# Moving the decoder bias of a fused attention and mixture-of-experts layer from a matmul to a VectorE add

## The chip, the cores and the metric

The kernel runs on one core of a Trainium2 chip. The metric is the device time of one execution in microseconds; of three runs the median counts. A profile of one further execution shows every instruction of every engine.

## The reference, cut to what matters

The layer takes `x` of 2 x 4096 tokens with 512 channels, normalizes it, and adds to `x` the output of a linear attention and that of a feed-forward branch with eight experts. The change concerns the end of the feed-forward branch:

```
moe_out = jnp.einsum('ned,ne->nd', eo, comb)
rates = jax.nn.sigmoid(moe_out @ c2s_w + c2s_b)
dec = jax.nn.sigmoid(x @ dec_w + dec_b)        # x is rates: 1024 -> 512
mu = jnp.mean(dec, axis=-1, keepdims=True)
var = jnp.var(dec, axis=-1, keepdims=True)
return (dec - mu) * jax.lax.rsqrt(var + 1e-05) * ln_g + ln_b
```

The bias `dec_b` runs along the 512 output channels, which lie in the free dimension of the output tile. The kernel computes both sigmoids as tanh of half the argument, so what it adds ahead of the second tanh is twice `dec_b` plus the sum of the decoder's weight rows. It has this row on all 128 partitions, once, at the start of the stage.

## The kernel before

Tokens are worked on in 16 blocks of 512 (four token tiles of 128). Four stages follow each other: `front` (A: normalization, encoder, router), `keyvalue` (B), `experts` (C) and `decode` (D). All matmuls of float32 data are done in passes over a high and a low part, so that one product is three matmuls. Each engine has its own instruction list, written out by hand, and waits on semaphores; nothing is reordered by a scheduler.

In `decode`, which the change touches, TensorE does for block i: four query projections (`query`, into banks `bX`), the transpose of the expert mixture (`middle`, L1443, waits for `mo`), content-to-rate products (`rates`, L1452 and L1453, into bank `bY`, wait for `midl`), the attention denominators, then the attention output of block i-1 (`attend`), then the decoder of block i: four bias matmuls (`decoder_bias`, L1494), and eight rounds `decoder(i, k)` of twelve matmuls into four banks `bD[t]`, between which stand `rates` for later rounds and the fan-out of the denominators (`fan`). The bias matmul multiplies a 128x128 selector by `rows`, a tile in which the high part of the bias row lies in partition 64 and its low part in partition 96.

ScalarE moves the queries (`q`, L1362, and `qh`, L1365), the mixture's high part (`midh`, L1370), the rates, and at the end of a block the four decoder banks with tanh into `out[:, t, :]` (L1421). VectorE does the low parts (`ql` L1564, `midl` L1569, `ratel` L1574), the shares `q` and `qnl` (L1609, L1614), the mixture of block i+1 (`half` L1548, `mo` L1555), and for block i-1 the statistics (`stats`, L1579 and L1584), the normalization (`norm` L1589), the residual (`add` L1597) and the sum with the attention output (`attend` L1604). Its order is that of the loop over blocks at the end of `decode`: the mixture of block i+1 is the last piece of block i's round, and the statistics of block i the first of the next. GpSimd gathers expert outputs and computes the inverse deviation; SyncE issues the loads and stores.

At the end of stage C, VectorE copies constants for stage D (L1260 to L1263).

Of the kernel before, what the change touches and what calls it, by code (L numbers as in the profile page):

```python
# [12 lines left out]
P = 128  # L13
# [94 lines left out]
def place(nc):  # L108
# [22 lines left out]
    put("CcD", "c2s", [P, HID], F32R)  # L131
    put("CcD", "fan", [P, KC, P], F32R)
    put("CcD", "rc2", [P, BLK], F32R)
    put("CcD", "rows", [P, BLK], F32R)
    put("CcD", "pick_bias", [P, P], F32R)
    put("CcD", "ln_g", [P, DIM])
    put("CcD", "bias", [P, DIM])
    for s in range(BATCH):
# [80 lines left out]
    put("Cc", "c2s_raw", [P, HID])  # L219
    put("Cc", "fanf", [P, KC, P])  # L220
    put("Cc", "blank", [P, BLK])
    put("Cc", "pbf", [P, P])
    put("Cc", "onesf", [MOE, BLK])
    put("Cc", "bias2", [P, 2, DIM])

# [3 lines left out]
    put("D", "rateh", [P, 3, BLK], F32R)  # L229
    put("D", "ratel", [P, 3, BLK], F32R)  # L230
    put("D", "out", [P, NT, DIM])
    put("D", "q", [P, KC, BLK])
    put("D", "qh", [P, 2, BLK], F32R)
    put("D", "ql", [P, 2, BLK], F32R)
# [796 lines left out]
def experts(nc, d, T, S):  # L1031
    with ExitStack() as ctx:
# [59 lines left out]

        @block.gpsimd
        def _(pool):
            fanf, pbf = T["fanf"], T["pbf"]
            pool.memset(T["onesf"][:, :], 1.0).then_inc(S["c_consts"], 1)
            pool.wait_ge(S["c_consts"], 1)
            pool.memset(T["blank"][:, :], 0.0).then_inc(S["c_consts"], 1)
            pool.memset(fanf[:, :, :], 0.0).then_inc(S["c_consts"], 1)
            pool.memset(pbf[:, :], 0.0).then_inc(S["c_consts"], 1)  # L1100
            pool.wait_ge(S["c_consts"], 4)
            pool.memset(fanf[0:MOE, :, :], 1.0).then_inc(S["c_consts"], 1)
            for k, row in enumerate((64, 96)):
                pool.wait_ge(S["c_consts"], 5 + k)
                pool.memset(pbf[row:row + 1, :], 1.0).then_inc(S["c_consts"], 1)
            n = 7
            for half in range(2):
                v = fanf[32 * half:32 * half + 32, :, :]
                for cm, st, base in ((-HD, 1, 0), (HD, -1, HD - 1)):
                    pool.wait_ge(S["c_consts"], n)  # L1110
                    pool.affine_select(out=v, in_=v, compare_op=ALU.is_ge, fill=0.0, base=base,
                                       pattern=[[st * P, KC], [st, P]], channel_multiplier=cm)\
                        .then_inc(S["c_consts"], 1)
                    n += 1
            pool.wait_ge(S["c_consts"], 11)
            pool.wait_ge(S["vec_in"], 32)
            pool.tensor_tensor(T["bias"][:, :], T["bias2"][:, 0, :], T["bias2"][:, 1, :], ALU.add)

# [101 lines left out]
        @block.vector  # L1220
        def _(dve):
            close_products(dve, T, S, 1)
            turn_dve(dve, T, S, 1, bY)
            dve.wait_ge(S["c_consts"], 1)
            for i in range(2):
                dve.tensor_copy(cl[MOE:P, i, :], T["onesf"][:, :]).then_inc(S["cl_ones"], 1)

            def content(g):
                dve.wait_ge(S["ch_out"], g + 1)
                if g >= 2:  # L1230
                    dve.wait_ge(S["e1_done"], (g - 2) * EC + EC)
                dve.tensor_tensor(cl[0:MOE, g % 2, :], bT[0:MOE, :], f32(ch[0:MOE, g % 2, :]), ALU.subtract)\
                    .then_inc(S["cl_out"], 1)

            def close_tile(g):
                dve.wait_ge(S["tout_done"], g + 1)
                wait(dve, S[f"eo_stored{g % 3}"], 16 * (g // 3))
                dve.tensor_reduce(yo[g % 3][:, :, :], bY[:, :].rearrange("p (t h c) -> p t c h", t=NT, h=2), AX.X, ALU.add)\
                    .then_inc(S["yo_out"], 1)

            for g in range(KC):
                project_dve(dve, T, S, 0, 1, g, bH[g])
            content(0)
            for n in range(LAST + LAG):
                g, j = divmod(n, EC)
                if j == 0 and g + 1 < NS:
                    content(g + 1)
                if n < LAST:
                    dve.wait_ge(S["hidh_out"], n + 1)
                    wait(dve, S["e2_done"], n - 3)  # L1250
                    dve.scalar_tensor_tensor(out=hidl[:, n % 4, :], in0=bH[n % 4][:, :], scalar=0.0,
                                             in1=f32(hidh[:, n % 4, :]), op0=ALU.max, op1=ALU.subtract)\
                        .then_inc(S["hidl_out"], 1)
                if j == 1 and g >= 2:
                    close_tile(g - 2)
                if j == 2 and g == 1:
                    close_denominators(dve, T, S, 0, 1)
                if j == 3 and g == 1:
                    dve.wait_ge(S["c_consts"], 11)
                    dve.tensor_copy(T["fan"][:, :, :], T["fanf"][:, :, :])  # L1260
                    dve.tensor_copy(T["pick_bias"][:, :], T["pbf"][:, :])
                    dve.tensor_copy(T["rc2"][:, :], T["blank"][:, :])
                    dve.tensor_copy(T["rows"][:, :], T["blank"][:, :]).then_inc(S["d_consts"], 1)  # L1263
                if j == 3 and 2 <= g < 2 + len(DEC):
                    name, c = DEC[g - 2]
                    dve.wait_ge(S["wh_out"], W_DEC + g - 1)
                    dve.tensor_tensor(T[name + "_l"][:, c, :], T[name + "_raw"][:, c, :], f32(T[name + "_h"][:, c, :]),
                                      ALU.subtract).then_inc(S["wl_out"], 1)
                if j == 3 and g == 16:
                    dve.wait_ge(S["wh_out"], W_C2S + 1)  # L1270
                    dve.tensor_tensor(T["c2s"][MOE:P, :], T["c2s_raw"][MOE:P, :], f32(T["c2s"][MOE:P, :]), ALU.subtract)\
                        .then_inc(S["wl_out"], 1)
            for g in range((LAST + LAG - 2) // EC - 1, NS):
                close_tile(g)
# [4 lines left out]
def decode(nc, d, T, S, out_dram):  # L1279
    with ExitStack() as ctx:  # L1280
# [4 lines left out]
        q, qh, ql, qnh, qnl = (T[n] for n in ("q", "qh", "ql", "qnh", "qnl"))  # L1285
        x = [T["xd0"], T["xd1"]]
        ga, gb, half, mo, midh, midl = (T[n] for n in ("ga", "gb", "half", "mo", "midh", "midl"))
        dlow, dsum, rc, rc2, rows = (T[n] for n in ("dlow", "dsum", "rc", "rc2", "rows"))

        block = ctx.enter_context(nc.Block())  # L1290

# [65 lines left out]
        def _(act):  # L1357
# [34 lines left out]
            for i in range(NB):  # L1392
# [22 lines left out]
                    if 3 <= k < 3 + KC:  # L1415
                        share(i, k - 3)
                for t in range(NT):
                    act.wait_ge(S["dec_done"], i * NT + t + 1)
                    if i:
                        act.wait_ge(S[f"stored{t}"], 16 * i)  # L1420
                    act.activation(out[:, t, :], bD[t][:, :], ACT.Tanh, scale=0.25).then_inc(S["dec_out"], 1)  # L1421

        @block.tensor
        def _(pe):
# [62 lines left out]
                    k = pe.matmul(bD[0][:, :], one, T["dec_l"][:, c, :], start=False, stop=(c == HC - 1))  # L1487
                k.then_inc(S["dec_summed"], 1)

            def decoder_bias(i, t):  # L1490
                if i == 0:
                    pe.wait_ge(S["rows_out"], 2)
                wait(pe, S["dec_out"], i * NT)
                pe.matmul(bD[t][:, :], T["pick_bias"][:, :], rows[:, :], start=True, stop=False)  # L1494

            def decoder(i, k):
                n = i * HC + k
                pe.wait_ge(S["ratel_out"], n + 1)
                for t in range(NT):
                    o = slice(t * P, (t + 1) * P)  # L1500
                    pe.matmul(bD[t][:, :], rateh[:, n % 3, o], T["dec_h"][:, k, :], start=False, stop=False)  # L1501
                    pe.matmul(bD[t][:, :], rateh[:, n % 3, o], T["dec_l"][:, k, :], start=False, stop=False)  # L1502
                    m = pe.matmul(bD[t][:, :], ratel[:, n % 3, o], T["dec_h"][:, k, :], start=False, stop=(k == HC - 1))  # L1503
                    if k == HC - 1:
# [4 lines left out]
            for i in range(NB + 1):  # L1509
# [20 lines left out]
                    for t in range(1, NT):  # L1530
                        attend(i - 1, t)
                if ahead:
                    for t in range(NT):
                        decoder_bias(i, t)
                    for k in range(HC):
                        decoder(i, k)
                        if k + 2 < HC:
                            rates(i, k + 2)
                        if 3 <= k < 3 + KC:
                            fan(i, k - 3)  # L1540

        @block.vector
        def _(dve):
# [27 lines left out]
            def rates(i, k):  # L1571
                n = i * HC + k
                dve.wait_ge(S["rateh_out"], n + 1)
                dve.tensor_tensor(ratel[:, n % 3, :], rate[:, k % 2, :], f32(rateh[:, n % 3, :]), ALU.subtract)\  # L1574
                    .then_inc(S["ratel_out"], 1)

            def stats(i, t):
                dve.wait_ge(S["dec_out"], i * NT + t + 1)
# [37 lines left out]
            def decoder_sum():  # L1616
                dve.wait_ge(S["dec_summed"], 1)
                dve.wait_ge(S["vec_in"], 48)
                dve.scalar_tensor_tensor(out=out[:, 0, :], in0=out[:, 1, :], scalar=2.0, in1=bD[0][:, :],
                                         op0=ALU.mult, op1=ALU.add).then_inc(S["dec_biased"], 1)  # L1620
                dve.wait_ge(S["dec_biased"], 1)
                dve.tensor_copy(rows[64:P, :], out[64:P, 0, :]).then_inc(S["rows_out"], 1)
                dve.wait_ge(S["rows_out"], 1)
                dve.tensor_tensor(rows[96:P, :], out[96:P, 0, :], f32(rows[96:P, :]), ALU.subtract)\
                    .then_inc(S["rows_out"], 1)

            for m in range(KC):
                query(0, m)
# [5 lines left out]
            for i in range(NB + 1):  # L1634
# [42 lines left out]
                if ahead:  # L1677
                    for k in range(HC):
# [6 lines left out]
                        if 3 <= k < 3 + KC:  # L1685
                            share(i, k - 3)
                            share_low(i, k - 3)
                        if k == HC - 1 and i + 1 < NB:
                            mixture(i + 1)


def build(nc, d, out_dram):
# [70 lines left out]
```

## Time and profile before

| what | us |
|---|---|
| three runs | 2024.8, 2026.44 (median), 2026.93 |
| the profiled execution | 2028.13 |
| its span, first to last instruction | 2026.4 |
| TensorE matmuls busy | 1965.3 (97%) |
| VectorE busy | 1045.1 (52%) |
| ScalarE busy | 814.9 (40%) |
| GpSimd busy | 392.9 (19%) |

The mean granted TensorE clock is 0.991 of full. Stage D begins near 1155 us. Busy shares are averages over stages; what bounds a stage is read from who waits for whom in it. A matmul's duration overlaps that of the next one, so what a matmul takes of TensorE's time is the distance of starts. "Idle before" in square brackets is the time that the engine stood still ahead of an instruction, with what released it.

### The profile page before, as it was taken

What the parts mean: (1) busy time and instruction counts of PE and PEld (TensorE: products, weight loads), DVE (VectorE), ACT (ScalarE), POOL (GpSimd) and SP (SyncE); (2) the same over time, 40 slices, a digit from 0 to 9 for tenths busy, and PEclk for the clock granted to TensorE, in tenths of its full rate; (3) what the DMA queues carried; (4) which work ended last, traced back from release to release, by engine and by line L of the source; (5) the groups of instructions that cost most, each with busy time, mean ns of one, the idle gap of its engine ahead of it and who ended that gap; (6) DMA issues with size and microseconds to landing.
All of it is one profiled execution on the core that took longest, in us unless ns stands there. A gap on an engine that the chain in (4) does not pass through costs nothing. (4 is left out here: it accounts for less than half of the span.)

```text
span 2026.4 us, 25149 instructions
## 1 busy us (share of the span) xinstructions
PE 1965.3 (97%) x9100; PEld 1609.1 (79%) x9100; DVE 1045.1 (52%) x1846; ACT 814.9 (40%) x1359; POOL 392.9 (19%) x428
## 2 busy tenths in 40 slices
PE   7999999999899999998899989999999999999998
PEld 5888888888788888887678768888888888888886
DVE  5445455553442222222888645555556556566554
ACT  4444445444221222112677533444344443444442
POOL 1000000000003444431000122222222222222220
PEclk9999999999999999999999989999999999999999
DMA  5561324423112233321877512222222222222210
GB/s 200 209 236 69 141 90 145 169 89 122 69 65 99 110 112 113 112 107 54 317 232 236 187 49 89 89 88 89 88 88 88 88 88 78 73 78 78 84 66 34
DMA packets 74826, 233.95 MB, mean 115 GB/s; under 512 B 9856, under 2 KB 15952, under 8 KB 68176
## 3 DMA queue, kind: packets, MB, share of 16 engines
q1 hardware_dynamic: 66432, 219.58, 30.7%
q0 software_dynamic: 8272, 12.76, 2.2%
q8 instruction: 73, 1.20, 0.2%
q14 instruction: 49, 0.40, 0.1%
HBM read 151.95 MB, written 80.36 MB: 115 GB/s over the span
## 5 line engine op out<-in xcount | busy, mean ns | idle before, releaser
L569 DVE TENSOR_TENSOR spl<-sp_t,sph 128x512 fp32r<-128x512 f32 x128 | 88.6, 692 | 240.1 <-ACT sph L391 240.1
L103 PE MATMUL A_E<-xs,enc_h 128*128 128x512 f32 x512 | 206.8, 404 | 0.0
L105 PE MATMUL A_E<-xs,enc_h 128*128 128x512 f32 x512 | 200.8, 392 | 0.0
L1574 DVE TENSOR_TENSOR ratel<-rate,rateh 128x512 fp32r<-128x512 f32 x128 | 88.5, 691 | 217.4 <-ACT rateh L1384 177.4
L104 PE MATMUL A_E<-xs,enc_l 128*128 128x512 f32 x512 | 200.6, 392 | 0.0
L1501 PE MATMUL D_D<-dec_h,rateh 128*128 128x512 f32 x512 | 199.8, 390 | 0.0
L1502 PE MATMUL D_D<-dec_l,rateh 128*128 128x512 f32 x512 | 199.8, 390 | 0.0
L1503 PE MATMUL D_D<-dec_h,ratel 128*128 128x512 f32 x512 | 199.5, 390 | 0.0
L1376 ACT ACTIVATE rate<-D_Y,cols 128x512 f32<-128x512 f32 x128 | 87.9, 687 | 264.3 <-PE D_Y L1453 261.5
L387 ACT ACTIVATE sp_t<-A_E,cols 128x512 f32<-128x512 f32 x128 | 88.1, 688 | 245.4 <-PE A_E L105 245.4
L863 POOL DMA_INDIRECT slots_scratch<-ctok,idx x128 | 123.8, 967 | 249.3 <-DVE v L991 123.4
L1333 POOL DMA_INDIRECT ga<-eo_scratch,idx x64 | 66.4, 1037 | 371.5 <-DVE ratel L1574 192.4
L991 DVE SCALAR_TENSOR_TENSOR v<-B_KV,v 128x512 fp32r<-128x512 f32 x64 | 44.3, 692 | 174.9 <-ACT v L892 174.8
L892 ACT ACTIVATE v<-B_KV 128x512 fp32r<-128x512 f32 x64 | 38.4, 600 | 204.8 <-PE B_KV L940 204.8
L1346 POOL TENSOR_TENSOR xd<-xd,bias 128x512 f32<-128x512 f32 x64 | 80.5, 1283 | 176.2 <-DVE out L1604 176.2
L105 PEld LDWEIGHTS A_E<-xs,enc_h 128*128 128x128 f32 x512 | 96.5, 189 | 21.6
L1502 PEld LDWEIGHTS D_D<-dec_l,rateh 128*128 128x128 f32 x512 | 96.2, 188 | 20.6
L1503 PEld LDWEIGHTS D_D<-dec_h,ratel 128*128 128x128 f32 x512 | 96.1, 188 | 20.5
L1501 PEld LDWEIGHTS D_D<-dec_h,rateh 128*128 128x128 f32 x512 | 96.3, 188 | 20.3
L103 PEld LDWEIGHTS A_E<-xs,enc_h 128*128 128x128 f32 x512 | 96.8, 189 | 19.0 <-issue 0.4
L104 PEld LDWEIGHTS A_E<-xs,enc_l 128*128 128x128 f32 x512 | 97.0, 189 | 18.6
L985 DVE SCALAR_TENSOR_TENSOR kl<-B_KV,kh 128x512 fp32r<-128x512 f32 x64 | 44.3, 692 | 128.5 <-ACT kh L888 128.5
(283 smaller groups left out, 4810.3 us busy)
## 6 DMA issues: line engine op xcount, KB each, us to landing
xs_scratch<-xs SPq DMA_DIRECT2D x16, 2048.0 KB, 9.3
xsd<-xs_scratch SPq DMA_DIRECT2D x16, 2048.0 KB
xs<-xs_scratch SPq DMA_DIRECT2D x14, 2048.0 KB, 8.5
wt<-ew_scratch SPq DMA_DIRECT2D x39, 513.0 KB, 3.8
x<-in_x SPq DMA_DIRECT2D x16, 1024.0 KB, 5.9
xd<-in_x SPq DMA_DIRECT2D x16, 1024.0 KB
out_y<-out SPq DMA_DIRECT2D x64, 256.0 KB, 2.1
slots_scratch<-zt SPq DMA_DIRECT2D x1, 9984.0 KB
```

Of the source, the lines that this page charges most:

```text
L103: pe.matmul(out, w_hi, x_hi, start=start, stop=False)
L104: pe.matmul(out, w_lo, x_hi, start=False, stop=False)
L105: return pe.matmul(out, w_hi, x_lo, start=False, stop=stop)
L387: act.activation(T["sp_t"][:, m % 2, :], bE[m % 2][:, :], ACT.Tanh, bias=T["enc_b"][:, m:m + 1], scale=0.5).then_inc(S["sp_out"], 1)
L569: dve.tensor_tensor(T["spl"][:, n % 3, :], T["sp_t"][:, m % 2, :], f32(T["sph"][:, n % 3, :]), ALU.subtract)\
L863: pool.indirect_dma_start(d["slots"][:, :], bass.IndirectOffsetOnAxis(ap=T["idx2" if second else "idx1"][:, t:t + 1], axis=0), T["ctok"][: ...
L1346: pool.tensor_tensor(x[i % 2][:, t, :], x[i % 2][:, t, :], T["bias"][:, :], ALU.add)\
L1376: act.activation(rate[:, k % 2, :], bY[:, :], ACT.Tanh, bias=T["c2s_b"][:, k:k + 1], scale=0.5)\
L1501: pe.matmul(bD[t][:, :], rateh[:, n % 3, o], T["dec_h"][:, k, :], start=False, stop=False)
L1502: pe.matmul(bD[t][:, :], rateh[:, n % 3, o], T["dec_l"][:, k, :], start=False, stop=False)
L1503: m = pe.matmul(bD[t][:, :], ratel[:, n % 3, o], T["dec_h"][:, k, :], start=False, stop=(k == HC - 1))
L1574: dve.tensor_tensor(ratel[:, n % 3, :], rate[:, k % 2, :], f32(rateh[:, n % 3, :]), ALU.subtract)\
```

## The change

The four bias matmuls of each block go. The first decoder matmul of each bank now starts the accumulation (`start=(k == 0)`), and waits until VectorE has emptied the bank for the block before. VectorE adds the bias row `dec_row` (128x512, the same row on all partitions) while it moves the bank into `out[:, t, :]` (`decoded`), and ScalarE's tanh reads and writes `out[:, t, :]` in SBUF. The wait for the store of the block before moves from ScalarE to VectorE with the write. `decoder_sum` writes `dec_row` in one operation; the two that split the row go, and so do the tiles `rows` and `pick_bias` and what fills them in stage C.

```
-            def decoder_bias(i, t):
-                if i == 0:
-                    pe.wait_ge(S["rows_out"], 2)
-                wait(pe, S["dec_out"], i * NT)
-                pe.matmul(bD[t][:, :], T["pick_bias"][:, :], rows[:, :], start=True, stop=False)
...
+                    if k == 0:
+                        if i:
+                            pe.wait_ge(S["biased"], (i - 1) * NT + t + 1)
+                        elif t == 0:
+                            pe.wait_ge(S["row_out"], 1)
-                    pe.matmul(bD[t][:, :], rateh[:, n % 3, o], T["dec_h"][:, k, :], start=False, stop=False)
+                    pe.matmul(bD[t][:, :], rateh[:, n % 3, o], T["dec_h"][:, k, :], start=(k == 0), stop=False)
...
+            def decoded(i, t):
+                dve.wait_ge(S["dec_done"], i * NT + t + 1)
+                if i == 0:
+                    dve.wait_ge(S["row_out"], 1)
+                else:
+                    dve.wait_ge(S[f"stored{t}"], 16 * i)
+                dve.tensor_tensor(out[:, t, :], bD[t][:, :], T["dec_row"][:, :], ALU.add).then_inc(S["biased"], 1)
...
-                    act.wait_ge(S["dec_done"], i * NT + t + 1)
-                    if i:
-                        act.wait_ge(S[f"stored{t}"], 16 * i)
-                    act.activation(out[:, t, :], bD[t][:, :], ACT.Tanh, scale=0.25).then_inc(S["dec_out"], 1)
+                    act.wait_ge(S["biased"], i * NT + t + 1)
+                    act.activation(out[:, t, :], out[:, t, :], ACT.Tanh, scale=0.25).then_inc(S["dec_out"], 1)
...
-                dve.scalar_tensor_tensor(out=out[:, 0, :], in0=out[:, 1, :], scalar=2.0, in1=bD[0][:, :],
-                                         op0=ALU.mult, op1=ALU.add).then_inc(S["dec_biased"], 1)
-                dve.wait_ge(S["dec_biased"], 1)
-                dve.tensor_copy(rows[64:P, :], out[64:P, 0, :]).then_inc(S["rows_out"], 1)
-                dve.wait_ge(S["rows_out"], 1)
-                dve.tensor_tensor(rows[96:P, :], out[96:P, 0, :], f32(rows[96:P, :]), ALU.subtract)\
-                    .then_inc(S["rows_out"], 1)
+                dve.scalar_tensor_tensor(out=T["dec_row"][:, :], in0=out[:, 1, :], scalar=2.0, in1=bD[0][:, :],
+                                         op0=ALU.mult, op1=ALU.add).then_inc(S["row_out"], 1)
...
-                        if k == HC - 1 and i + 1 < NB:
-                            mixture(i + 1)
+                        if k == HC - 1:
+                            if i + 1 < NB:
+                                mixture(i + 1)
+                            for t in range(NT):
+                                decoded(i, t)
...
-                    dve.tensor_copy(T["pick_bias"][:, :], T["pbf"][:, :])
-                    dve.tensor_copy(T["rc2"][:, :], T["blank"][:, :])
-                    dve.tensor_copy(T["rows"][:, :], T["blank"][:, :]).then_inc(S["d_consts"], 1)
+                    dve.tensor_copy(T["rc2"][:, :], T["blank"][:, :]).then_inc(S["d_consts"], 1)
```

On VectorE, at the end of a block's round and the start of the next one, this is the order before (`half` and `mo` are the mixture, `st` and `mv` the statistics, `midl` the low part that TensorE's `rates` needs):

```order
L1614 TENSOR_TENSOR qnl<-q,qnh 128x512
L1548 TENSOR_SCALAR half<-ga,w_60 128x64 x4
L1555 SCALAR_TENSOR_TENSOR mo<-gb,w_61,half 128x128 x4
L1579 BN_STATS st<-out 128x6 x4
L1582 MEMSET held 128x1
L1584 BN_AGGR mv<-st 128x2 x4
L1589 SCALAR_TENSOR_TENSOR out<-out,mv,ln_g 128x512
L1564 TENSOR_TENSOR ql<-q,qh 128x512
L1569 TENSOR_TENSOR midl<-D_Y,midh 128x512
```

And the same place after the change (line numbers have moved by a few):

```order
L1609 TENSOR_TENSOR qnl<-q,qnh 128x512
L1535 TENSOR_SCALAR half<-ga,w_60 128x64 x4
L1542 SCALAR_TENSOR_TENSOR mo<-gb,w_61,half 128x128 x4
L1570 TENSOR_TENSOR out<-D_D,dec_row 128x512 x4
L1574 BN_STATS st<-out 128x6 x4
L1577 MEMSET held 128x1
L1579 BN_AGGR mv<-st 128x2 x4
L1584 SCALAR_TENSOR_TENSOR out<-out,mv,ln_g 128x512
L1551 TENSOR_TENSOR ql<-q,qh 128x512
L1556 TENSOR_TENSOR midl<-D_Y,midh 128x512
```

Four adds from the banks stand between the mixture and the statistics; the rest keeps its order.

On TensorE, where the attention output of block i-1 ends and the decoder of block i begins, before:

```order
L1478 MATMUL D_X<-mh_78,qnh 128x512
L1479 MATMUL D_X<-ml_79,qnh 128x512
L1480 MATMUL D_X<-mh_78,qnl 128x512
L1494 MATMUL D_D<-rows,pick_bias 128x512 x4
L1501 MATMUL D_D<-dec_h,rateh 128x512
```

And after:

```order
L1468 MATMUL D_X<-mh_76,qnh 128x512
L1469 MATMUL D_X<-ml_77,qnh 128x512
L1470 MATMUL D_X<-mh_76,qnl 128x512
L1490 MATMUL D_D<-dec_h,rateh 128x512
L1491 MATMUL D_D<-dec_l,rateh 128x512
```

The four matmuls of `rows` and `pick_bias` are gone, and the first decoder round follows the attention output directly.

## Rows read from the trace of the kernel before

**Rows 1.** Waits of TensorE in stage D: us in total, times, longest us.

```profile
PE D_Y L1452 <- DVE midl L1569: 9.7, 16, 1.4
PE D_X L1478 <- DVE out L1604: 4.7, 1, 4.7
PE D_Y L1443 <- DVE mo L1555: 3.8, 1, 3.8
```

**Rows 2.** TensorE in order of time, at a block boundary: start us, us, what.

```profile
1432.80 0.50 PE L1452 MATMUL D_Y<-midh,c2s 128*128 128x512 f32 x1 [0.56 <-DVE midl L1569]
```

**Rows 3.** VectorE in order of time, at the same boundary.

```profile
1425.53 0.69 DVE L1614 TENSOR_TENSOR qnl<-q,qnh 128x512 fp32r<-128x512 f32 x1 [0.70 <-ACT qnh L1390]
...
1426.79 1.13 DVE L1555 SCALAR_TENSOR_TENSOR mo<-gb,w,half 128x128 f32<-128x128 f32 x4
1427.84 2.47 DVE L1579 BATCH_NORM_STATS2 st<-out 128x6 f32<-128x512 f32 x4
...
1432.07 0.68 DVE L1569 TENSOR_TENSOR midl<-D_Y,midh 128x512 fp32r<-128x512 f32 x1
1432.67 0.73 DVE L1597 SCALAR_TENSOR_TENSOR out<-out,rs,xd 128x512 f32<-128x512 f32 x1
```

**Rows 4.** ScalarE in order of time, at the same boundary.

```profile
1425.40 2.04 ACT L1421 ACTIVATE out<-D_D 128x512 f32<-128x512 f32 x4
...
1430.21 0.58 ACT L1370 ACTIVATE midh<-D_Y 128x512 fp32r<-128x512 f32 x1
```

**Rows 5.** TensorE in order of time, at the bias matmuls of two blocks.

```profile
1187.81 1.91 PE L1494 MATMUL D_D<-rows,pick_bias 128*128 128x512 f32 x4
1189.52 0.51 PE L1501 MATMUL D_D<-dec_h,rateh 128*128 128x512 f32 x1
...
1399.46 1.07 PE L1494 MATMUL D_D<-rows,pick_bias 128*128 128x512 f32 x4
1400.37 0.39 PE L1501 MATMUL D_D<-dec_h,rateh 128*128 128x512 f32 x1
```

**Rows 6.** VectorE in order of time, last block, two adds from a bank.

```profile
2015.19 1.28 DVE L1604 TENSOR_TENSOR out<-D_X,out 128x512 f32<-128x512 f32 x2
```

**Rows 7.** TensorE in order of time, at three longer waits.

```profile
964.12 0.47 PE L1193 MATMUL C_H<-ch,wt 128*128 128x512 f32 x1 [1.61 <-issue]
...
1171.58 0.50 PE L1460 MATMUL D_Y<-qh,den 128*128 128x512 f32 x1 [2.21 <-DVE ql L1564]
...
1172.61 0.55 PE L1486 MATMUL D_D<-dec_h,ones 128*128 128x512 f32 x1
...
2015.93 0.79 PE L1478 MATMUL D_X<-mh,qnh 128*128 128x512 f32 x1 [4.70 <-DVE out L1604]
2016.52 0.63 PE L1479 MATMUL D_X<-ml,qnh 128*128 128x512 f32 x1
```

**Rows 8.** Stretches: A:B length, busy us by engine, granted clock, DMA share, GB/s.

```profile
2016.00:2019.00 3.00, 3.00 (x7) 2.41 (x8) 0.48 (x1) 0.00 (x0) 0.00 (x0) 0.50 0.47 175
...
1172.70:1176.00 3.30, 3.30 (x10) 2.53 (x9) 0.00 (x0) 0.00 (x0) 0.00 (x0) 0.50 0.98 415
...
964.00:967.00 3.00, 2.08 (x10) 1.44 (x10) 1.09 (x3) 1.70 (x4) 0.00 (x0) 1.00 1.04 406
```

**Rows 9.** VectorE and TensorE in order of time: constants' copies, bias row split.

```profile
975.48 0.21 DVE L1261 CAST pick_bias<-pbf 128x128 fp32r<-128x128 f32 x1
975.62 0.42 DVE L1262 CAST rc<-blank 128x512 fp32r<-128x512 f32 x1
975.95 0.41 DVE L1263 CAST rows<-blank 128x512 fp32r<-128x512 f32 x1
...
977.61 0.50 PE L1202 MATMUL C_O<-hidh,wt 128*128 128x512 f32 x1 [0.92 <-DVE hidl L1251]
...
1178.33 0.42 DVE L1622 CAST rows<-out 64x512 fp32r<-64x512 f32 x1
1178.79 0.69 DVE L1624 TENSOR_TENSOR rows<-out,rows 32x512 fp32r<-32x512 f32 x1
```

More of the change, by code:

```diff
@@ L133, in place @@
     put("CcD", "rc2", [P, BLK], F32R)
-    put("CcD", "rows", [P, BLK], F32R)
-    put("CcD", "pick_bias", [P, P], F32R)
     put("CcD", "ln_g", [P, DIM])
@@ L221, in place @@
     put("Cc", "blank", [P, BLK])
-    put("Cc", "pbf", [P, P])
     put("Cc", "onesf", [MOE, BLK])
@@ L231, in place @@
     put("D", "out", [P, NT, DIM])
+    put("D", "dec_row", [P, DIM])
     put("D", "q", [P, KC, BLK])
@@ L1094, in _ @@
         def _(pool):
-            fanf, pbf = T["fanf"], T["pbf"]
+            fanf = T["fanf"]
             pool.memset(T["onesf"][:, :], 1.0).then_inc(S["c_consts"], 1)
@@ L1099, in _ @@
             pool.memset(fanf[:, :, :], 0.0).then_inc(S["c_consts"], 1)
-            pool.memset(pbf[:, :], 0.0).then_inc(S["c_consts"], 1)
-            pool.wait_ge(S["c_consts"], 4)
+            pool.wait_ge(S["c_consts"], 3)
             pool.memset(fanf[0:MOE, :, :], 1.0).then_inc(S["c_consts"], 1)
[L1103 to L1106, printed above, removed]
+            n = 4
             for half in range(2):
@@ L1114, in _ @@
                     n += 1
-            pool.wait_ge(S["c_consts"], 11)
+            pool.wait_ge(S["c_consts"], 8)
             pool.wait_ge(S["vec_in"], 32)
@@ L1258, in _ @@
                 if j == 3 and g == 1:
-                    dve.wait_ge(S["c_consts"], 11)
+                    dve.wait_ge(S["c_consts"], 8)
                     dve.tensor_copy(T["fan"][:, :, :], T["fanf"][:, :, :])
-                    dve.tensor_copy(T["pick_bias"][:, :], T["pbf"][:, :])
-                    dve.tensor_copy(T["rc2"][:, :], T["blank"][:, :])
-                    dve.tensor_copy(T["rows"][:, :], T["blank"][:, :]).then_inc(S["d_consts"], 1)
+                    dve.tensor_copy(T["rc2"][:, :], T["blank"][:, :]).then_inc(S["d_consts"], 1)
                 if j == 3 and 2 <= g < 2 + len(DEC):
@@ L1287, in decode @@
         ga, gb, half, mo, midh, midl = (T[n] for n in ("ga", "gb", "half", "mo", "midh", "midl"))
-        dlow, dsum, rc, rc2, rows = (T[n] for n in ("dlow", "dsum", "rc", "rc2", "rows"))
+        dlow, dsum, rc, rc2 = (T[n] for n in ("dlow", "dsum", "rc", "rc2"))
         block = ctx.enter_context(nc.Block())
@@ L1532, in _ @@
                 if ahead:
-                    for t in range(NT):
-                        decoder_bias(i, t)
                     for k in range(HC):
```

## Prediction

> **What bounds the kernel now.** I read the table of engines, then the waits of TensorE in the last stage, then one block boundary in order of time on TensorE, VectorE and ScalarE, and last the stretches of half clock. TensorE is busy nearly everywhere; in the last stage, where the change is, it waits in few places [rows 1]. Sixteen times it waits for VectorE's `midl` (9.7 us in all), once 3.8 us for `mo` (first block) and once 4.7 us for `out` (after the last block). Inside a block its stream has no holes. So a matmul taken out of the stream gives its whole period back, and anything that makes `midl` later is paid in full, because TensorE already stands there with nothing in hand.
>
> At the boundary of blocks 4 and 5 TensorE has drained its projections and waits 0.56 us before the first content-to-spike matmul L1452 at 1432.80 [rows 2]. It waits for `midl`, which VectorE starts at 1432.07 and ends at 1432.75 [rows 3]. Before that VectorE runs without a pause from 1425.53: the last `qnl`, the mixture, four `bn_stats`, aggregation, `norm`, `ql`, `midl`. ScalarE is no rival releaser: `midh`, the input of `midl`, ends at 1430.79 [rows 4], 1.28 us before `midl` starts. What holds `midl` back is VectorE's own queue. The other boundaries repeat this, with waits of about 0.6 us (9.7 us less the first block's 1.4, over 15).
>
> **What is removed.** The four bias matmuls at the start of a block's decoder. They take from 1399.46 to 1400.37, 0.91 us, or 0.227 us each, since matmuls overlap and the 0.39 us of one is not its price [rows 5]. Fifteen blocks give 15 x 0.91 = 13.6 us; the first block's four run at half clock, from 1187.81 to 1189.52, and give 1.7. Nothing else on TensorE changes: the first decoder matmul of a tile now opens the sum. Removed: 15.3 us.
>
> The Trainium skill, page "TensorE: Matmul & The Clock Gate", section "Back-to-back issue gap", gives about 131 ns as the sustained spacing of matmuls with 512 columns. By it 64 of them would be an estimated 8.4 us and the sum would come out 6.9 us later; the trace disagrees with its 227 ns, and the trace has these very matmuls, so the measurement decides.
>
> **What is added.** Four VectorE adds a block, bank and SBUF row in, `out` tile out, put behind the mixture and ahead of the next block's work. Their nearest row is the add L1604, which reads a bank and a tile of the same shape: two of them back to back take 1.28 us, one alone 0.69, so they start 0.59 to 0.60 us apart [rows 6]. Four move everything behind them by 4 x 0.60 = 2.40 us. Bounds from the rows: a 128x512 copy starts 0.34 us after the one ahead of it [rows 9] (four: 1.36 us), and 0.73 us is the `scalar_tensor_tensor` behind `midl`, close to an unoverlapped 0.69 (four: 2.9 us). I take 2.40.
>
> The Trainium skill, page "VectorE: DVE Perf Modes", section "The DRAIN you can't avoid", has it that the next operation does not start until the pipeline of the one before is empty. By that rule the four adds would be 4 x 0.69 = 2.76 us, an estimate, and fifteen boundaries would be 5.4 us more; the two adds in 1.28 us speak against it.
>
> Can anything cover the 2.40 us? The adds could have begun earlier, since three of the four tiles are summed before the last `qnl` ends, but in VectorE's order they stand behind the mixture, where the engine has not one idle slice before `midl`. Their inputs are long ready, so no new wait for TensorE enters. Behind them are queued the four statistics, which now wait for a tanh that waits for an add. The first tanh starts about 0.7 us after the first add, takes 0.6 and is done about 1.1 us before the first statistic's turn, so the round trip costs nothing more. ScalarE has the four tanhs, until now done at 1427.4, held to about 1431.0 on the same scale; then come `q`, `qh` and `midh`, which ends near 1432.7, still 1.8 us ahead of where `midl` now starts (1434.47). ScalarE stays off the path. The waits on `stored` move from ScalarE to VectorE; they name stores issued behind the attention output of the block before, ahead of the whole decoder, and are long fulfilled.
>
> So at each of 15 boundaries TensorE's wait of 0.56 us becomes 2.96 us: +2.40 x 15 = +36.0 us. Everything in a block shifts with its start, so the 0.91 us won does not shorten the wait.
>
> **What the longer wait does to the clock.** After a wait of 4.70 us in the last block the granted clock is 0.50 (1.2 GHz), and 7 matmuls take 3.00 us, 0.43 each [rows 7, 8]; after one of 2.21 us it fell too, though only 1.0 us after work had begun again; after one of 1.61 us it stayed at 1.00 (2.4 GHz). The 0.56 us waits never cost it. A half-clock stretch costs: from 2016 to 2019, 7 matmuls x (0.43 - 0.227) = 1.4 us, with its edges about 1.5. A wait of 2.96 us lies above the 2.21 that did it and below 4.70. I take 12 of 15 boundaries, as where the wait falls seems to matter: 12 x 1.5 = +18 us. Bounds: none, and 15 x 1.7 = 25.
>
> **The ends.** First block: the two operations that split the bias row (1178.33 and 1178.79 [rows 9]) go, together 1.2 us of the chain that TensorE's 3.8 us wait hangs on: -1.2. In the last block the 4.7 us wait for `out` grows by the same four adds: +2.4; its half-clock stretch may last a little longer (0 to 1.5). In the expert stage two constant copies go, 0.14 and 0.34 us apart from their neighbours, just ahead of a 0.92 us wait [rows 9]: at most -0.5, I take -0.3. The three small fills on GpSimd are off the path.
>
> **Sum**, against the profiled execution (2028.13 us, span 2026.4 and 1.7 around it): -15.3 + 36.0 + 18.0 - 1.2 + 2.4 - 0.3 = +39.6, so 2067.7. The median of the runs is 2026.44, 1.7 below the profiled one; the median forecast is 2066 us.
>
> **Rivals.**
> *The clock holds.* The wait grows as said, but at 2.96 us the half clock comes rarely. For it: the last stage shows no wait between 2.21 and 3.8 us, so the price at 2.96 is not seen. Then -15.3 + 36.0 - 1.2 + 2.4 - 0.3 = +21.6: 2048 us. Chance 0.2.
> *The clock stays low longer.* In the first block, waits of 3.8 and 1.4 us [rows 1] stand close together, and the bias matmuls at 1187.81 behind both still ran at half clock [rows 5]. If each boundary cost two stretches, another 15 x 1.5 = 22 us, or if the adds do not overlap (+5): 2070 to 2090, with a middle of 2084. Against it: TensorE has 10 us of unbroken matmuls right behind the wait. Chance 0.12.
> *The adds are covered (the other side).* One mechanism: VectorE's queue up to `midl` has room, so the adds fit in where it idles for `qnh` (0.70 us before 1425.53). It decides where the four adds delay `midl` by less than the 0.91 us that the matmuls give back, 0.23 us an add, which is under even the 0.34 us of a copy. Wholly covered it would give 2026.4 - 15.3 - 1.5 = 2010 us. Against it: the written order, which puts them behind `qnl`. Chance 0.06.
> *A draw.* A cover of some 1.5 us a boundary and no clock loss lands within 0.2% (4 us, about what can be told from no change): 0.03.
>
> **How the numbers follow.** Forecast 0.59, clock holds 0.2, clock low longer 0.12, covered 0.06, draw 0.03. The likeliest case alone runs from 2056 (half of the boundaries lose the clock) to 2076 (all at 1.7, adds at 0.65). The range takes in the clock rival at 2048 with slack for cheaper adds, and the lower part of the slow rival: 2044 to 2080. Faster 0.06, same 0.03, slower 0.91.
>
> **What would show it.** In the changed kernel's profile: TensorE's wait for `midl` at 15 boundaries near 3.0 us, 45 us in all where it was 9.7; VectorE's adds 0.60 us apart right behind `mo`; `midh` done before `midl` starts; a block from decoder start to boundary 0.91 us shorter; stretches of granted clock 0.50 behind most boundaries, each 1.5 us dear; a last wait for `out` near 7.1 us. It would be wrong if the wait for `midl` stayed under 1.5 us, if ScalarE's `midh` or `qh` released VectorE there, or if the clock row stayed at 9 throughout.

## The result: 2.8% slower

The changed kernel takes 2082.96 us (median of five runs, 2081.44 to 2089.77) against 2026.93 us; the ratio is 1.028 with a 95% interval of 1.0263 to 1.0297. The forecast was 2066 us in a range of 2044 to 2080. The direction and the chain of causes were right; the time lies 3 us beyond the range, and one term of the sum was too small.

The waits of TensorE in stage D of the changed kernel (us in total, times, longest us) answer to [rows 1]:

```profile
PE D_Y L1442 <- DVE midl L1556: 45.5, 16, 3.0
PE D_X L1468 <- DVE out L1599: 7.0, 1, 7.0
...
PE D_Y L1433 <- DVE mo L1542: 2.5, 1, 2.5
```

The wait for `midl` went from 9.7 to 45.5 us, that for the last `out` from 4.7 to 7.0, that for the first `mo` from 3.8 to 2.5. These three differences are +35.8, +2.3 and -1.3 us; the forecast had +36.0, +2.4 and -1.2.

VectorE at one boundary of the changed kernel, in order of time, which answers to [rows 3]:

```profile
1437.26 0.69 DVE L1609 TENSOR_TENSOR qnl<-q,qnh 128x512 fp32r<-128x512 f32 x1 [0.70 <-ACT qnh L1382]
...
1438.52 1.13 DVE L1542 SCALAR_TENSOR_TENSOR mo<-gb,w,half 128x128 f32<-128x128 f32 x4
1439.57 2.47 DVE L1570 TENSOR_TENSOR out<-D_D,dec_row 128x512 f32<-128x512 f32 x4
1441.96 2.46 DVE L1574 BATCH_NORM_STATS2 st<-out 128x6 f32<-128x512 f32 x4
...
1446.18 0.68 DVE L1556 TENSOR_TENSOR midl<-D_Y,midh 128x512 fp32r<-128x512 f32 x1
```

From the end of the mixture to the first statistic there are now 1441.96 - 1439.57 = 2.39 us: the adds start 0.60 us apart. ScalarE's high part is no releaser, as forecast, with 1.8 us to spare:

```profile
1440.28 2.42 ACT L1411 ACTIVATE out<-out 128x512 f32<-128x512 f32 x4 [3.06 <-DVE out L1570]
...
1443.76 0.58 ACT L1362 ACTIVATE midh<-D_Y 128x512 fp32r<-128x512 f32 x1
```

What the forecast undersized stands behind the wait. TensorE at this boundary, and at the one before it, in order of time, answers to [rows 2, 7]:

```profile
1389.95 0.79 PE L1442 MATMUL D_Y<-midh,c2s 128*128 128x512 f32 x1 [2.94 <-DVE midl L1556]
1390.55 0.63 PE L1443 MATMUL D_Y<-midl,c2s 128*128 128x512 f32 x1
...
1395.67 0.61 PE L103 MATMUL D_X<-xsd,wq_h 128*128 128x512 f32 x1
1396.09 0.42 PE L104 MATMUL D_X<-xsd,wq_l 128*128 128x512 f32 x1
...
1446.92 0.50 PE L1442 MATMUL D_Y<-midh,c2s 128*128 128x512 f32 x1 [2.96 <-DVE midl L1556]
1447.25 0.56 PE L1443 MATMUL D_Y<-midl,c2s 128*128 128x512 f32 x1
...
1450.59 0.47 PE L105 MATMUL D_X<-xsd,wq_h 128*128 128x512 f32 x1
1450.90 0.40 PE L103 MATMUL D_X<-xsd,wq_h 128*128 128x512 f32 x1
```

At the second of them the clock falls just after work has begun again (the first matmul takes 0.50 us, the second 0.56), and 9 matmuls take 3.65 us, from 1447.25 to 1450.90, where 9 x 0.23 = 2.1 would do: 1.6 us lost. At the first the clock has fallen 0.65 us before TensorE resumes (already its first matmul takes 0.79 us), and 14 matmuls take 6.14 us, from 1389.95 to 1396.09, for 3.2: 2.9 us lost. The stretches (length, busy us of TensorE, its weight loads, VectorE, ScalarE, GpSimd, then the granted clock, DMA share, GB/s) say the same:

```profile
1336.00:1340.00 4.00, 4.00 (x18) 3.27 (x18) 3.96 (x7) 1.51 (x3) 0.00 (x0) 1.00 0.00 0
1390.00:1396.00 6.00, 6.00 (x14) 4.74 (x15) 4.58 (x7) 1.32 (x2) 0.00 (x0) 0.50 0.00 0
...
1447.40:1450.60 3.20, 3.20 (x10) 2.43 (x9) 3.16 (x6) 1.32 (x2) 0.00 (x0) 0.50 0.01 3
1451.00:1455.00 4.00, 4.00 (x19) 3.24 (x18) 1.19 (x2) 2.44 (x4) 0.00 (x0) 1.00 0.00 0
```

Behind 14 of the 15 boundaries the clock fell to 0.50, that is 1.2 GHz (the one near 1336 kept it); eight times in the short form, six in the long one: 8 x 1.6 + 6 x 2.9 = 30 us, where the forecast had 18. The starts of the `rates` matmuls at four successive boundaries (1335.81, 1389.95, 1446.92 and 1502.63 us) give the same prices: the block behind the boundary that kept the clock takes 54.1 us, the one behind a long stretch 57.0, the one behind a short stretch 55.7.

### The profile page after: what moved, and what is told of

The parts are those of the page before. It is cut to its first block and busy times, and to the rows that moved or that the text cites. A ratio compares the mean times of both kernels' runs of the same rounds, so it can differ in the third digit from the quotient of the medians.

```text
span 2081.2 us, 25098 instructions
## 1 busy us (share of the span) xinstructions
PE 1983.4 (95%) x9036; PEld 1620.5 (78%) x9036; DVE 1081.3 (52%) x1906; ACT 818.7 (39%) x1359; POOL 388.7 (19%) x425
## 5 line engine op out<-in xcount | busy, mean ns | idle before, releaser
L103 PE MATMUL D_X<-xsd,wq_h 128*128 128x512 f32 x256 | 112.1, 438 | 3.0 <-PEq L1030 3.0
```

What stands on the lines that cost most here:

```text
L103: pe.matmul(out, w_hi, x_hi, start=start, stop=False)
```

## The experiments

Where a ratio is given, it is to the kernel before on the same chip in the same series, with a 95% interval. Beside the time I give the length of stage D in the profile, from the first transpose of the mixture (L1443 before, L1433 after) to the end of the span. It leaves out the three earlier stages, whose end varied between 1179.6 and 1185.2 us in the profiles taken here: before 845.0 us, changed 899.7. Each of these lengths is good to 0.1 us. Where I give the length of a block, it is the distance between the starts of the first `rates` matmul at successive boundaries, averaged over the 14 such distances from the second block on.

**The wait filled with work (e1_fill).** Ten matmuls nobody needs keep TensorE busy ahead of the wait:

```
             def rates(i, k):
+                if k == 0 and i:
+                    pe.wait_ge(S["qn_out"], i * KC)
+                    for _ in range(10):
+                        pe.matmul(bR[:, :], T["wq_h"][:, 0, 0:P], xs[:, 0, 0, :], start=True, stop=True)
                 pe.wait_ge(S["midl_out"], i + 1)
```

> The changed kernel with 10 more matmuls of 512 columns on TensorE just ahead of the wait for midl, at each of the 15 boundaries, into the bank bR that the next denominators overwrite. They take 10 x 0.227 = 2.3 us of a wait of 2.96 us. Theory (the wait costs its own length, and about 32 us more are half clock behind it): VectorE's chain ends at the same time, TensorE's wait falls to about 0.7 us, and the clock stays at 1.00 behind the boundaries; only the clock's share goes: 2083 - 30 = about 2052 us. Rival A (the overrun over the forecast is contention of the four adds with the matmuls, or anything else on VectorE's side): no change, 2080 to 2085. Rival B (the ten matmuls are paid as work): 2083 + 34 = 2117.

Measured: 2053.2 us, 1.0126 (1.0104 to 1.0148); stage D 869.9 us. Ten more matmuls a boundary made the kernel 30 us faster. TensorE's waits of this run, where 15 of the 16 waits for `midl` are now 0.6 us long:

```profile
PE D_Y L1446 <- DVE midl L1560: 10.5, 16, 1.4
PE D_X L1472 <- DVE out L1603: 7.0, 1, 7.0
```

and two stretches of it, the first across one boundary, the second from the end of the first block's half clock to the last block, across all 15:

```profile
1389.00:1396.00 7.00, 6.40 (x28) 4.89 (x27) 6.33 (x11) 2.89 (x6) 1.80 (x2) 1.00 0.00 1
...
1195.30:2041.50 846.20, 832.77 (x3639) 674.90 (x3637) 521.91 (x890) 339.02 (x546) 224.01 (x212) 1.00 0.22 76
```

The clock column reads 1.00 in both. VectorE's chain is as late as in the changed kernel: a block takes 54.2 us here, and 54.1 there behind the one boundary that kept the clock. So it is the clock that gave the 30 us back: 899.7 - 869.9 = 29.8. Contention and "matmuls are paid as work" both fall as explanations.

**Fewer of them (e8_fill_six).** The same with `range(6)`.

> The changed kernel with 6 more matmuls ahead of the wait for midl, where the first such run had 10. Nothing on VectorE's side changes, so the boundary is as long; TensorE's own wait is about 2.96 - 6 x 0.23 = 1.6 us. Theory (the clock's loss hangs on how long TensorE stands still, and 1.6 us is not enough): full clock behind the boundaries, the same time as with ten, about 2053 us. Rival (it takes less than that, and ten matmuls only just sufficed): half clock behind most of them at 1.6 us each, 2070 to 2078 us.

Measured: 2052.15 us, 1.0125 (1.0108 to 1.0141); stage D 869.2 us.

```profile
PE D_Y L1446 <- DVE midl L1560: 24.5, 16, 1.6
...
1188.70:2035.00 846.30, 819.16 (x3579) 663.74 (x3578) 521.42 (x889) 338.84 (x546) 220.91 (x212) 1.00 0.22 76
```

Waits of 1.5 us at the boundaries (24.5 us less the first block's 1.4, over 15) left the clock at full: the second line is the stretch across all of them. The time is that of ten fillers.

**The removal alone (e2_no_add).** No `decoded`; the tanh reads the bank as before, and the bias is left out. TensorE's wait ahead of the first decoder matmul names the tanh instead of the add, here and in the kernels with fewer adds.

```
-                            for t in range(NT):
-                                decoded(i, t)
...
-                    act.wait_ge(S["biased"], i * NT + t + 1)
-                    act.activation(out[:, t, :], out[:, t, :], ACT.Tanh, scale=0.25).then_inc(S["dec_out"], 1)
+                    act.wait_ge(S["dec_done"], i * NT + t + 1)
+                    if i:
+                        act.wait_ge(S[f"stored{t}"], 16 * i)
+                    act.activation(out[:, t, :], bD[t][:, :], ACT.Tanh, scale=0.25).then_inc(S["dec_out"], 1)
```

> The changed kernel without the four adds: the bias row is left out of the decoder, and ScalarE's tanh reads the bank as before. This is the removal of the matmuls alone. Theory (a matmul in the full stream gives back its period of 0.227 us): 2027 - 15.3 - 1.3 = 2010 us, TensorE's waits for midl back at 0.6 us. Rival (a removed matmul is worth less, for instance 0.131 us, or its gain is lost in the wait for midl): 2017 to 2025 us.

Measured: 2014.5 us, 0.9944 (0.9922 to 0.9966); stage D 831.1 us. The time lies between the theory and the rival. By the ratio the gain is 11.3 us (6.9 to 15.8), less than the 16.6 expected. By the trace stage D is 845.0 - 831.1 = 13.9 us shorter, and the wait for `mo`, ahead of it, 1.3 us: together 15.2. A block shrinks from 52.7 to 51.8 us, by 0.90, which is four matmuls of 0.225. The waits for `midl` are exactly those of before, 9.7 us. The price of 0.227 us a matmul is borne out by the trace; the runs alone would not tell it from a somewhat smaller one.

**The addition alone (e4_before_adds).** The kernel before, and four adds at the same place that nobody reads:

```
-                        if k == HC - 1 and i + 1 < NB:
-                            mixture(i + 1)
+                        if k == HC - 1:
+                            if i + 1 < NB:
+                                mixture(i + 1)
+                            for t in range(NT):
+                                dve.wait_ge(S["dec_out"], i * NT + t + 1)
...
+                                dve.tensor_tensor(ql[:, t % 2, :], bD[t][:, :], T["ln_g"][:, :], ALU.add)\
+                                    .then_inc(S["spared"], 1)
```

> The kernel before, bias matmuls kept, with four further VectorE adds behind the mixture; each reads a decoder bank and writes a tile that nobody reads. This is the addition alone. Theory (the two parts add up): changed kernel + 15.3 + 1.3 = about 2099 us, waits for midl near 2.96 us, 15 of them; the clock share may differ by some 8 us, as it depends on where the waits fall. Rival (in the changed kernel it is the longer round trip add, tanh, statistics that costs, not the adds' place in VectorE's queue): here tanh does not wait for an add, so the wait stays well below 2.96 us and the time near 2060.

Measured: 2096.6 us, 1.0347 (1.0325 to 1.037); stage D 915.3 us.

```profile
PE D_Y L1452 <- DVE midl L1571: 45.4, 16, 3.0
PE D_X L1478 <- DVE out L1606: 7.1, 1, 7.1
```

The same 45 us of waits without any tanh waiting for an add; the clock fell at all 15 boundaries, at seven of them in the long form. The kernel also makes VectorE and TensorE wait for these adds before they reuse the tile and the bank. With four adds it is the place in VectorE's queue that costs, and removal and addition add up: 2096.6 - 2083.0 = 13.6.

**Two adds, one add, three adds (e3_two_adds, e3c_one_add, e3b_three_adds).** Only the first two, one or three tiles are moved by VectorE; the tanh of the others reads its bank:

```
+                    if t < 2:
+                        act.wait_ge(S["biased"], i * 2 + t + 1)
+                        act.activation(out[:, t, :], out[:, t, :], ACT.Tanh, scale=0.25).then_inc(S["dec_out"], 1)
+                        continue
...
-                            for t in range(NT):
+                            for t in range(2):
                                 decoded(i, t)
```

> The changed kernel with the add on two of the four token tiles only; the other two tiles get no bias, their tanh reads the bank. Theory (0.60 us of wait for each add, half clock only behind waits above some 2 us): wait for midl 0.56 + 1.20 = 1.76 us, clock at 1.00 behind nearly all boundaries: 2010 + 15 x 1.20 + 1.2 = about 2030 us. Rival (each add costs the same, the clock included, a straight line from no add to four): (2010 + 2083) / 2 = 2046 us.

> The changed kernel with the add on one token tile only; the other three get no bias. With two adds the wait was 1.95 us and 12 of 15 boundaries were followed by half clock. Theory (a wait well below 1.6 us leaves the clock alone): wait about 1.3 us, no half clock behind the boundaries, 2014.5 + 15 x 0.75 + 0.8 = about 2027 us. Rival (the clock falls behind any wait longer than the 0.56 us of before): 15 x 1.6 more, about 2050.

> The changed kernel with the add on three token tiles; the fourth gets no bias. Wait about 2.5 us. Theory (how long the clock stays down grows with the wait: with two adds 12 stretches of one length, with four adds 14, six of them twice as long): nearly all boundaries, one to four of them doubled: 2014.5 + 15 x 1.95 + 1.8 + 15 x 1.6 + 4 = about 2073 us. Rival (a stretch of half clock costs the same 1.5 us whatever the wait, and the changed kernel's doubled ones are chance): none doubled, about 2067.

Measured: 2055.4 us with two, 2056.6 with one, 2057.0 with three (stage D 872.0, 873.2 and 873.0). All three expectations missed, theory and rival alike: one add costs as much as three. The wait was 1.95 us with one add as with two, where 1.3 and 1.76 us had been expected; half clock followed that length too; and with three adds it came more rarely than with one. The waits for `midl`, of two, one and three adds in turn:

```profile
PE D_Y L1448 <- DVE midl L1562: 30.6, 16, 2.0
```

```profile
PE D_Y L1448 <- DVE midl L1562: 30.7, 16, 2.0
```

```profile
PE D_Y L1448 <- DVE midl L1562: 36.9, 16, 2.4
```

VectorE with one add, in order of time, shows why:

```profile
1380.25 0.69 DVE L1576 TENSOR_TENSOR out<-D_D,dec_row 128x512 f32<-128x512 f32 x1
1381.63 2.47 DVE L1580 BATCH_NORM_STATS2 st<-out 128x6 f32<-128x512 f32 x4 [0.70 <-ACT out L1412]
```

Behind the add VectorE stands idle for 0.70 us, until the tanh that waited for the add is done: 0.69 + 0.70 = 1.39 us for the round trip, less than which no number of adds on the first tiles can cost. With four adds the round trip lies under the other three. The wait of 0.56 + 1.39 = 1.95 us was followed by half clock at 12 of 15 boundaries with two adds, at 13 with one, in the short form each time. With three adds the wait is 2.37 us and yet only 9 boundaries lost the clock, so that the longer wait and the fewer losses come out even. Whether a given boundary loses it is not a matter of the wait's length alone.

The trace shows a pattern in it. With one and two adds a block takes 53.2 us where the clock holds and 54.7 where it falls, with three adds 53.6 and 55.1; the mean is 54.5, 54.5 and 54.4 us. In all three runs successive falls lie 54.6 us apart, or twice that where one boundary between them was spared. With two adds the first fall comes 1.3 us after TensorE resumed, each further one about 0.1 us earlier, the last 0.03 us after; at the next boundary there is none. This suggests that a boundary is lost or spared by where its wait lies against these 54.6 us, and that the mean block comes out at nearly that for this reason, whether it holds one add or three. No run varied it by itself, and what sets the distance of the falls these runs do not show.

**The one add on the last tile (e7_add_on_last).**

```
-                            for t in range(NT):
-                                decoded(i, t)
+                            decoded(i, NT - 1)
```

> The changed kernel with one add, on the last token tile instead of the first; the other three get no bias. With the add on the first tile the wait was 1.95 us, since VectorE stood idle for 0.70 us until the tanh behind its add was done. Theory (one add costs 0.60 us of VectorE's queue, and the round trip add, tanh, statistics costs extra only where the first statistic waits for it; half clock follows waits of 1.95 us but not of 1.6): the round trip now hides behind the first three statistics, wait 1.16 us, no half clock behind the boundaries, 2014.5 + 15 x 0.60 + 0.6 = about 2024 us. Rival (it is having any add there at all that costs 40 us): as with one add on the first tile, 2056 us.

Measured: 2025.75 us, 0.9989 (0.9979 to 0.9999); stage D 841.3 us, against 831.1 without adds and 873.2 with the add on the first tile. TensorE's waits for `midl`, and VectorE at a boundary:

```profile
PE D_Y L1448 <- DVE midl L1562: 18.6, 16, 1.4
...
1372.10 0.68 DVE L1576 TENSOR_TENSOR out<-D_D,dec_row 128x512 f32<-128x512 f32 x1
1372.69 2.46 DVE L1580 BATCH_NORM_STATS2 st<-out 128x6 f32<-128x512 f32 x4
```

The waits at the boundaries are 1.15 us long (18.6 less 1.4, over 15), as expected, and none was followed by half clock. On VectorE 0.59 us lie between the starts and nothing is idle. The same single add costs 10 us on the last tile and 42 us on the first: 15 x 0.8 of round trip and some 20 of clock are the difference.

**The low part first (e5_midl_first).** If the place in the queue is the cause, another order must cure it. VectorE makes `ql` and `midl` right behind the adds, and ScalarE makes `q`, `qh` and `midh` of the next block behind its first tanh:

```
                     act.activation(out[:, t, :], out[:, t, :], ACT.Tanh, scale=0.25).then_inc(S["dec_out"], 1)
+                    if t == 0 and i + 1 < NB:
+                        query(i + 1, 0)
+                        middle(i + 1)
...
+                if ahead and behind:
+                    query(i, 0)
+                    middle(i)
                 if behind:
                     for t in range(NT):
                         stats(i - 1, t)
                     norm(i - 1, 0)
                 if ahead and behind:
-                    query(i, 0)
-                    middle(i)
+                    query(i, 1)
...
```

> The changed kernel in another order: VectorE makes the low parts ql and midl of the next block right behind the four adds, ahead of the statistics, and ScalarE moves q, qh and midh behind its first tanh and ahead of the other three; the low part of the second query is pulled ahead of one norm and of the two residual adds. Theory (the adds cost only because they stand ahead of midl in VectorE's queue): midl ends before TensorE asks for it, the 15 waits of 2.96 us go and with them the half clock; 2027 - 15.3 (matmuls) - 8.4 (the 0.56 us waits) - 1.3 + 2.4 (tail) = about 2004 us, faster than the kernel before. Rival (VectorE has no room for four more operations at a boundary, wherever they stand): the wait moves to a low part of a later query or to the attention sum, and the time stays above 2040.

Measured: 2002.72 us, 0.9874 (0.9859 to 0.9889); stage D 820.3 us. This version beats the kernel before by 1.26%. VectorE at a boundary:

```profile
1418.89 2.48 DVE L1571 TENSOR_TENSOR out<-D_D,dec_row 128x512 f32<-128x512 f32 x4
1421.43 0.69 DVE L1552 TENSOR_TENSOR ql<-q,qh 128x512 fp32r<-128x512 f32 x1
1422.04 0.68 DVE L1557 TENSOR_TENSOR midl<-D_Y,midh 128x512 fp32r<-128x512 f32 x1
1422.64 2.46 DVE L1575 BATCH_NORM_STATS2 st<-out 128x6 f32<-128x512 f32 x4
```

and TensorE there, which uses `midl` in L1443 and no longer waits for it:

```profile
1422.90 0.39 PE L105 MATMUL D_X<-xsd,wq_h 128*128 128x512 f32 x1
1423.13 0.40 PE L1443 MATMUL D_Y<-midh,c2s 128*128 128x512 f32 x1
```

`midl` ends at 1422.72 and is asked for at 1423.13. The adds fill time in which VectorE would otherwise wait for `qh`; how much, the next run shows.

**The same order with the bias matmuls (e6_midl_first_matmul).** The control: both reorderings on the kernel before.

> The kernel before, with the bias matmuls, in the same new order of VectorE and ScalarE. Control for the run above. Theory: only the 0.56 us waits at 15 boundaries go: 2027 - 8.4 = about 2018 us, some 14 us above the run above, which is the matmuls' price less the tail's 2.4. Rival (the order alone is what helps, and the place of the bias does not matter): the same time as the run above.

Measured: 2014.8 us, 0.9932 (0.9919 to 0.9946); stage D 831.9 us, 13.1 less than before. Without the four adds VectorE stands idle for 2.40 us at the same place, about what they take:

```profile
1426.75 0.69 DVE L1565 TENSOR_TENSOR ql<-q,qh 128x512 fp32r<-128x512 f32 x1 [2.40 <-ACT qh L1365]
```

The 0.56 us waits are gone (8.4), and the last wait for `out` is 3.9 us for 4.7. The remaining 4 us come from the waits too. This is TensorE at a boundary of the kernel before:

```profile
1431.85 0.40 PE L105 MATMUL D_X<-xsd,wq_h 128*128 128x512 f32 x1
1432.80 0.50 PE L1452 MATMUL D_Y<-midh,c2s 128*128 128x512 f32 x1 [0.56 <-DVE midl L1569]
1433.14 0.39 PE L1453 MATMUL D_Y<-midl,c2s 128*128 128x512 f32 x1
```

and at one of this run:

```profile
1428.27 0.39 PE L105 MATMUL D_X<-xsd,wq_h 128*128 128x512 f32 x1
1428.49 0.40 PE L1453 MATMUL D_Y<-midh,c2s 128*128 128x512 f32 x1
1428.73 0.39 PE L1454 MATMUL D_Y<-midl,c2s 128*128 128x512 f32 x1
```

From the first to the third start there are 1.29 us before and 0.46 here. The wait is listed with 0.56 us and costs 0.83, because the matmuls on its two sides do not overlap: 15 x 0.27 = 4 us more. A block is 0.84 us shorter than before (51.85 against 52.69).

The rival is out: against the run above, 2014.8 - 2002.7 = 12.1 us, and a block takes 51.85 us here and 50.96 there, 0.89 less. Once the adds stand where they delay nobody, the change is worth what its matmuls cost, less the 2.4 us by which the last wait for `out` is longer (6.3 against 3.9).

## Why the forecast was wrong

The step that failed is the term of the sum for the half clock behind the boundaries, "12 x 1.5 = +18 us". The runs show 29.8 us in its place. It was undersized in both factors. The clock fell at 14 of 15 boundaries and not at 12; and a fall that comes early enough in the wait costs 2.9 us, not 1.5.

At 1.5 us each the two further boundaries make 3 us, and the six long stretches make 8 more than six short ones; about 0.8 us lie in the last block. The 12 itself stood on no row, and the runs with two and three adds show that such a count can't be read off the wait's length.

The rows of before show no long stretch behind a single wait: in the one of the last block [rows 7] it was of the short form. But the trace of before has long stretches at the starts of stages, where two waits stand close together, as here, with half clock until 961 us:

```profile
954.79 1.11 PE L741 MATMUL C_Y<-ident,numm 128*128 128x128 f32 x4 [3.46 <-DVE numm L693]
957.31 0.79 PE L103 MATMUL C_H<-wp_h,vth 128*128 128x512 f32 x1 [1.41 <-DVE vtl L717]
...
954.30:961.00 6.70, 4.80 (x13) 3.63 (x14) 3.42 (x6) 1.79 (x3) 3.77 (x9) 0.50 0.90 301
```

They say that a second length exists, though not that one wait is enough for it.

The bounds that the text gave for this term (none to 25 us) were themselves too narrow, since its upper end was 15 short stretches. The rival "the clock stays low longer" named a middle of 2084 us by two stretches at each boundary; what happened is a mixture of it and the forecast, six boundaries in the long form and eight in the short. One smaller slip: the lower end of the likeliest case, half of the boundaries at 1.5 us, is 2066 - 18 + 11 = 2059 us and not 2056.

The other terms, stage by stage:

| term | forecast | measured | from |
|---|---|---|---|
| bias matmuls | -15.3 | -13.9 in stage D | e2_no_add |
| adds, 15 boundaries | +36.0 | +35.8 | waits for `midl` |
| adds, tail | +2.4 | +2.3 | wait for `out` |
| first block | -1.2 | -1.3 | wait for `mo` |
| clock | +18 | +29.8 | e1_fill |

The first line counts the clock of the tail too, so it is not quite the matmuls alone: by the block lengths 15 blocks give 13.5 us, as forecast, and the first block's 1.7 us could not be told apart from the tail. The text left the last block's half clock out of its sum ("0 to 1.5"); in the changed kernel 14 matmuls start there before the clock is full again, before it was 8, some 1.2 us. The sum of the measured terms is +52.7 us; the spans differ by 54.8, and some 1.4 us of the rest arose ahead of stage D, in stages where the change does next to nothing (both profiles begin the first transposes at 1181.4 and 1181.5 us, though the changed kernel waited 1.3 us less for `mo`). The last 0.7 us I did not trace.

Right were: that `midl` and VectorE's own order bound the boundary, that ScalarE stays off it, that the adds overlap at 0.60 us apart (2.39 us for four, where the flat rule of the Trainium skill's page "VectorE: DVE Perf Modes", section "The DRAIN you can't avoid", would have given an estimated 2.76; the same section adds that an operation that is not held starts earlier, and the trace agrees with that), and that the block's gain of 0.91 us does not shorten the wait. One sentence was right only for this case: that the round trip add, tanh, statistics "costs nothing more". With four adds it is covered; with one on the first tile it costs 0.70 us on top of the add's 0.69.

## What to carry to other kernels

Before work is moved to an engine that is idle half of the time, look at which of its instructions the bound engine waits for, and where in its list the new ones stand: here four adds cost 68 us where they stand ahead of `midl` (2083.0 against 2014.5), and after a reordering they delay it no longer. A wait on TensorE had a second price in the clock behind it, with four adds nearly as large as the added wait itself, and it came in steps, not in proportion. Filling the wait with matmuls that nobody needs gave 30 us back, though that kernel is still slower than the one before (2053 against 2027 us); removing the wait by the other order is what made the change pay. An engine that hands a tile to another and needs it back should have other work in between, as the last tile had and the first had not.

## What the runs showed of the hardware

Waits of 1.5 us on TensorE, 15 of them (e8_fill_six), never brought the granted clock down; waits of 1.95 us did at 12 and 13 of 15 boundaries, of 2.37 us at 9, of 2.96 us at 14, and at all 15 in the kernel before with the adds. The half-clock stretch behind one had two forms, 1.6 and 2.9 us dear, the second only where the fall came 0.6 us or more ahead of TensorE's next matmul (all six in the changed kernel, 0.65 to 0.78 us ahead; in the kernel before with the adds seven long ones, 0.60 to 0.90 ahead, and four short ones of falls 0.45 to 0.58 ahead). A wait of 0.56 us between matmuls cost 0.83 us of TensorE's time, since the matmuls on its two sides do not overlap. The Trainium skill, page "TensorE: Matmul & The Clock Gate", section "Why this matters for your kernels", warns of idle gaps between bursts of matmuls, and puts the harmful length well above the 1.95 us that sufficed here; the measurement decides. Which boundary is spared goes with where its wait lies against falls that come 54.6 us apart with one, two and three adds; what sets that distance was not settled.
